# Masked scores written to the ring of probabilities in SBUF, with the exponentials in place there

## The reference, cut to what matters

```
# layer 0: 32 query heads of 16, 8 key/value heads, mask added, bias on every projection
scores = q @ k.T * 16**-0.5 + mask          # 32 x [100, 361]
x = layernorm(softmax(scores) @ v @ Wo + bo + x)
# layer 1: 16 heads of 32 on the normalized context, boolean mask
x = x + tanh(gate) * (softmax(where(mask, q @ k.T * 32**-0.5, -inf)) @ v @ Wo)
```

## Time and profile before

| | us |
|---|---|
| median of 3 executions | 1225.03 |
| the profiled execution, device time | 1223.34 |
| its span in the profile | 1221.5 |
| TensorE matmul busy | 1148.4 (94%) |
| VectorE busy | 806.6 (66%) |
| ScalarE busy | 759.1 (62%) |
| granted TensorE clock, mean | 0.993 |

### The profile page before, as it was taken

The page is one execution under the profiler, slowest core; times in us unless marked ns, Lnnn a source line. Parts: engine busy times, 40 slices in busy tenths (PEclk is TensorE's granted clock), DMA queues, the critical chain, the costliest instruction groups (busy, mean ns, idle before and its releaser), DMA issues.

```text
span 1221.5 us, 32246 instructions
## 1 busy us (share of the span) xinstructions
PE 1148.4 (94%) x10003; PEld 942.6 (77%) x10003; DVE 806.6 (66%) x2370; ACT 759.1 (62%) x2179; POOL 251.6 (21%) x264
## 2 busy tenths in 40 slices
PE   4899999999999999999999999999999999999997
PEld 4678687787878878787887878778787878878786
DVE  4465667667577675757777675767767576675735
ACT  3464756757475675747567474766747476574744
POOL 1042212111121211113121121312122131211210
PEclk9799999999999999999999999999999999999999
DMA  7774627447362744736365482635647273564500
GB/s 237 193 174 99 159 70 173 109 103 190 77 170 69 159 126 101 187 72 163 86 138 147 89 197 64 171 87 127 155 91 189 63 168 91 125 164 94 135 15 8
DMA packets 77965, 153.77 MB, mean 126 GB/s; under 512 B 10528, under 2 KB 47200, under 8 KB 77296
## 3 DMA queue, kind: packets, MB, share of 16 engines
q1 hardware_dynamic: 77936, 153.40, 51.9%
HBM read 113.72 MB, written 39.65 MB: 126 GB/s over the span
## 4 chain that ended last, share of the span: by engine, by line
PE 72%; issue 11%; ACT 7%; DVE 4%; DMA 2%; DVEq 1%; ACTq 1%; SPq 1%; POOL 1%; POOLq 0%
PE PJ L365 16%; PE TP L416 14%; PE SCO L402 6%; PE OA L436 6%; PE SCO L682 5%; PE SCO L460 5%; PE PJ L468 5%; PE PJ L378 4%; ACT PR L1048 3%; PE OA L441 3%; PE SCO L365 2%; ACT PT L1059 2%; DVE SCO L819 2%; PE SCO L406 2%; DVE MN L819 1%
## 5 line engine op out<-in xcount | busy, mean ns | idle before, releaser
L1048 ACT ACTIVATE PR<-SCO,MN 100x361 f32<-100x361 f32 x768 | 426.2, 566 | 147.4 <-DVE MN L819 143.8
L819 DVE CUSTOM_DVE_ANT_0 SCO<-SCO,MK 100x361 f32<-100x361 f32 x768 | 403.0, 550 | 134.8 <-PE SCO L402 102.7
L416 PEld LDWEIGHTS TP<-ident,PR 100*128 100x128 f32 x2304 | 223.1, 141 | 86.8 <-ACT PT L1059 36.9
L416 PE MATMUL TP<-ident,PR 100*128 100x100 f32 x2304 | 270.2, 253 | 10.6 <-ACT PT L1059 4.8
L1059 ACT ACTIVATE PT<-TP 121x600 f32<-121x600 f32 x256 | 171.8, 671 | 49.6 <-PE TP L416 45.7
L402 PE MATMUL SCO<-K0S,Q0S 128*100 128x362 f32 x512 | 161.7, 371 | 32.3 <-ACT PR L1048 26.5
L1048 ACT ACTIVATION_READ_ACCUMULATOR PR<-SCO,MN 100x1 f32 x768 | 158.8, 207 | 0.0
L829 DVE COPY PT<-TP 121x600 f32<-121x600 f32 x128 | 100.1, 782 | 48.8 <-PE TP L416 46.0
L402 PEld LDWEIGHTS SCO<-K0S,Q0S 128*100 128x100 f32 x512 | 74.6, 166 | 56.4 <-ACT PR L1048 47.6
L819 DVE DVE_READ_ACCUMULATOR2_ANT MN<- 100x1 f32 x768 | 109.6, 143 | 0.0
L1217 POOL TENSOR_TENSOR K1F<-K1F,KB 128x364 f32<-128x364 f32 x64 | 50.7, 793 | 279.4 <-DVE K1F L811 278.1
(11 more groups left out here) (140 smaller groups left out, 1813.4 us busy)
## 6 DMA issues: line engine op xcount, KB each, us to landing
K1S<-k_scr SPq DMA_DIRECT2D x128, 364.0 KB, 6.2
k_scr<-K1HL SPq DMA_DIRECT2D x64, 364.0 KB, 2.9
Q0S<-q_scr SPq DMA_DIRECT2D x128, 100.0 KB, 3.9
K0S<-k_scr SPq DMA_DIRECT2D x64, 182.0 KB, 5.0
AT<-ctx_cols SPq DMA_DIRECT2D x16, 722.0 KB, 9.4
V<-ctx_rows SPq DMA_DIRECT2D x16, 484.0 KB
q_scr<-QHL SPq DMA_DIRECT2D x16, 400.0 KB, 2.5
k_scr<-K1HL SPq DMA_DIRECT2D x32, 182.0 KB, 3.0
```

The costliest lines, as they stand in the source:

```text
L416: last = pe.transpose(TP[:, k % 2, c * T:(c + 1) * T], PR[0:T, k % NPR, c * SP:c * SP + P], ident[0:T, 0:T])
L819: dve.tensor_tensor_reduce(out=bank, in0=bank, in1=mask[0:T, :], scale=scale, scalar=3.4e38, op0=ALU.add, op1=ALU.min, accum_out=MN[0:T, k ...
L1048: act.activation(PR[0:T, k % NPR, 0:S], SCO[0:T, k % 3, 0:S], ACT.Exp, bias=MN[0:T, k:k + 1], scale=-1.0, accum_out=SM[0:T, k:k + 1]).then ...
```

## The change

`shift` writes its masked scores into `PR` in SBUF and no longer back into the PSUM bank. It takes over ScalarE's wait for the transposes of pair p - 3. `exps` reads and writes the same buffer of `PR`. TensorE's waits on a bank of `SCO` now ask for the maximum of the tile three before (`shifted`) and not for its exponential (`prob`). VectorE waits once, ahead of its batches, for the zeros that GpSimd puts into `PR`. No line of the diff touches the place of VectorE's copies.

```diff
@@ TensorE, layer 0 (L589)
                         if k >= 3 or not first:
-                            pe.wait_ge(prob, NH * b + k - 2)
+                            pe.wait_ge(shifted, NH * b + k - 2)
                         score(b, k)
@@ TensorE, keys of the next sequence into bank 1 (L646)
-                    pe.wait_ge(prob, NH * b + 32)
+                    pe.wait_ge(shifted, NH * b + 32)
@@ TensorE, layer 1 (L716, L730)
-                        pe.wait_ge(prob, NH * b + 2 * p - 2)
+                        pe.wait_ge(shifted, NH * b + 2 * p - 2)
...
-                        pe.wait_ge(prob, NH * b + 2 * p - 1)
+                        pe.wait_ge(shifted, NH * b + 2 * p - 1)
@@ VectorE, shift (L813)
                 dve.wait_ge(scored, NH * b + k + 1)
+                wait_from(dve, pt_mm, NPAIR * b + k // 2 - 2)
                 dve.sem_inc(met_dve, 1)
-                bank = SCO[0:T, k % 3, 0:S]
                 mask, scale = (MK0, -1.0) if k < 32 else (MK1, -SCALE1)
-                dve.tensor_tensor_reduce(out=bank, in0=bank, in1=mask[0:T, :], scale=scale, scalar=3.4e38,
+                dve.tensor_tensor_reduce(out=PR[0:T, k % NPR, 0:S], in0=SCO[0:T, k % 3, 0:S], in1=mask[0:T, :],
+                                         scale=scale, scalar=3.4e38,
                                          op0=ALU.add, op1=ALU.min, accum_out=MN[0:T, k:k + 1]).then_inc(shifted, 1)
@@ VectorE, ahead of batch 0
+            dve.wait_ge(pool_zero, 3)
@@ ScalarE, exps (L1045)
                 act.wait_ge(shifted, NH * b + k + 1)
-                wait_from(act, pt_mm, NPAIR * b + k // 2 - 2)
-                act.activation(PR[0:T, k % NPR, 0:S], SCO[0:T, k % 3, 0:S], ACT.Exp, bias=MN[0:T, k:k + 1],
+                act.activation(PR[0:T, k % NPR, 0:S], PR[0:T, k % NPR, 0:S], ACT.Exp, bias=MN[0:T, k:k + 1],
                                scale=-1.0, accum_out=SM[0:T, k:k + 1]).then_inc(prob, 1)
```

## The result

The changed kernel takes 1253.8 us (median of 4, 1252.7 to 1254.6) against 1224.9 us for the kernel before on the same chip. The ratio is 1.024, with a 95% interval of 1.022 to 1.025. It is 29 us slower; the forecast was 14 us faster.

The account below looks back on a forecast made before the run. TensorE, with matmuls busy 94% of the span, was taken as the bound. 1.13 - 0.48 + 0.45 - 0.15 = 0.95 us a sequence, times 14, plus 1.0 for batches 0 and 15, is 14.3 us: 1225.0 to 1211, range 1204 to 1218.

Parts of the forecast that it names:

- part (2) of what the change adds: Wait moved from ScalarE to VectorE: never the last met, costs 0 to 0.15 us at idle starts, taken as 0.05.
- Part (3): VectorE's wait for GpSimd's zeros is met long before its first maximum, and the keys' bank wait already was: cost 0.
- The slower rival: Extra wait not hidden on VectorE, 0.12 us on about 20 maxima a sequence: 21 us slower, 1246; chance 0.10.
- The stalls, one by one: Seven score stalls of the loop's sequence, each checked against the next copy wait: 0.40 + 0.46 + 0.40 - 0.13 = 1.13 us kept.
- layer 1: Ring of transposes, VectorE's copy, maximum, exponential and ScalarE's copy, with no score in it: stalls there keep nothing.
- output projection: Behind score 13: starts 0.86 us earlier, when layer 1's outputs are ready; 0.46 us kept in addition to 0.40.
- transposes 7: Behind score 19: of 0.54 us freed, 0.40 is kept, since copy 6 then holds them.
- transposes 9: They hang through ScalarE on maximum 20, which gains only 0.27 us: 0.13 of the 0.40 lost again.
- The waits for ScalarE's copies: Sign of being right: transposes' waits for ScalarE's copies rise from 36.9 us towards 70.
- Exponentials from SBUF: ScalarE's exponentials 30 ns longer each, 16 counting in a sequence: 0.48 us lost, bounds 0.14 and 1.22.
- the nine idle starts of the prediction: Exponentials 0, 4, 8, 16, 20, 24, 35, 40, 44, where idle ScalarE loses its wait: 0.05 us each, 0.45 gained.
- The waits: Per sequence, ScalarE gains 0.45 us at nine idle starts; VectorE loses 0.15 at three (maxima 0, 20 and 26).

Follow-up runs that it names:

- e2: Kernel before, with 20 semaphore increments that nobody waits for on VectorE's queue between batch 0 and its loop: 1267.6 us, ratio 1.035.
- e5: Kernel before, with 17 semaphore increments that nobody waits for ahead of VectorE's loop: 1226.8 us, ratio 1.001.
- e6: Whole changed kernel, with 70 idle increments far ahead in VectorE's queue, where it waits for the first weights: 1206.0 us, ratio 0.985.
- e8: Changed kernel without VectorE's wait for the transposes, and with TensorE's four bank waits set back from `shifted` to `prob`: 1219.0 us, ratio 0.996.
- e1: Changed kernel without VectorE's wait for the transposes, which TensorE's order already implies: 1201.7 us, ratio 0.981.
- e9: Kernel before, without ScalarE's implied wait for the transposes ahead of each exponential: 1219.3 us, ratio 0.996.
- e3: Changed kernel with 60 idle semaphore increments ahead of VectorE's loop: 1211.7 us, ratio 0.989.
- e7: Changed kernel with 40 idle increments far ahead in VectorE's queue, where it waits for the first weights: 1306.2 us, ratio 1.066.
- e4: Kernel before, with 17 idle increments inside VectorE's loop body, in a stretch where VectorE is idle: 1225.1 us, ratio 1.000.

## Why the prediction was wrong

*The failed step* is part (2) of what the change adds: that the moved wait "costs only its place in the queue", at most 0.15 us at a few idle starts. I counted its time and not its instructions, nor where they push the end of VectorE's loop. Part (3) did the same with the wait for GpSimd's zeros: met long before it is needed, it is still one of the two instructions that carry the end from 576 to 578. e2 shows that 20 instructions without any function do the same, e5 that 17 don't, e6 that the changed kernel without the stall takes 1206.0 us. The missing term is +47.8 us. Without slow matmuls the stall costs 73.03 - 70.57 = 2.46 us a pass, of which 2.10 us show as TensorE's wait; the slow matmuls behind eleven of the thirteen returns add 74.37 - 73.03 = 1.34 us each.

*The slower rival* named VectorE's wait and the range up to 1246, but by another mechanism, a price on each of about 20 maxima. It isn't what happened: the wait costs 4.3 us in all, 0.3 us a pass, and the loss sits at one place of a pass.

*The stalls, one by one.* e8 and e1 differ only in the bank waits. Times from the cast of the earlier trace rows on, in e8 and e1:

| point | e8 | e1 | gain | forecast |
|---|---|---|---|---|
| transposes 1 | 22.38 | 22.05 | 0.33 | 0.40 |
| transposes 3 | 26.39 | 26.06 | 0.33 | 0.40 |
| output projection | 28.00 | 27.13 | 0.87 | 0.86 |
| transposes 7 | 36.52 | 35.38 | 1.14 | 1.26 |
| transposes 9 | 40.13 | 39.00 | 1.13 | 1.13 |
| period | 71.39 | 70.24 | 1.15 | 1.13 |

This step was right, layer 1 included: transposes 21 start at 12.94 and 12.97. The waits for ScalarE's copies rose to 64.7 us in e1, where I had said towards 70.

*Exponentials from SBUF.* Drawn, they are 590 - 566 = 24 ns longer each, forecast 30. But two in a row, before and after, start further apart by more than that:

```profile
636.98 0.57 ACT L1048 ACTIVATE PR<-SCO,MN 100x361 f32<-100x361 f32 x1
...
637.52 0.57 ACT L1048 ACTIVATE PR<-SCO,MN 100x361 f32<-100x361 f32 x1
```

```profile
643.03 0.59 ACT L1050 ACTIVATE PR<-PR,MN 100x361 f32<-100x361 f32 x1
...
643.61 0.59 ACT L1050 ACTIVATE PR<-PR,MN 100x361 f32<-100x361 f32 x1
```

That is 0.54 and 0.58 us. Over all exponentials in a row it is 0.535 to 0.553 us before and 0.578 to 0.596 after, 43 ns more, which is the figure that the prediction gives beside its own 30. The cost on the path was mis-sized all the same: I took 0.48 us a pass and set VectorE's side at zero, with bounds of 0.02 us for a maximum, but its accumulator reads end 60 ns earlier. This saving reaches ScalarE: where that had been idle, the exponential starts 0.62 us after the start of its maximum in e9 and 0.57 in e8. At the nine idle starts of the prediction that would be about 0.5 us a pass, an estimate from these two numbers, and so about as much as the 0.48 us that I took for the exponentials. Together, e8 against e9, they gain no more than 0.13 us a pass. No run has one of the two without the other.

*The waits.* ScalarE's loss of its wait: forecast 0.45, measured 71.88 - 71.52 = 0.36. VectorE's wait: forecast 0.15, measured 0.28 (e3) to 0.33 (e6).

Without the stall the sum is 1.15 + 0.36 + 0.13 - 0.33 = 1.31 us a pass, which is 71.88 - 70.57, where I had 0.95; in all the change without the stall (e6) gains 18.9 us, where I had 14.3. The 0.95 was low mainly because the cost of the exponentials was counted and the gain from the accumulator reads wasn't.

## What to carry to other kernels

In a hardware loop, count instructions as well as their time: each wait against a loop's counter may bring an instruction of its own, and a body that comes to touch a third block of 256 instructions costs microseconds at every return, whatever the new instructions do. Instructions ahead of the loop count as well, because they move it. Idle time in the profile that ends with "issue" and occurs once a pass, together with more instruction packets, is the sign; moving the body by idle instructions ahead of it tells place from work. And look for waits that another engine's order already implies: dropping one was worth 5 us in the kernel before, and made the change 23 us faster instead of 29 us slower.

## What the runs showed of the hardware that I had not expected

- A boundary of VectorE's instruction fetch lies ahead of place 321 of its queue (e7) and another ahead of 577 or 578 (e4 and e5 against the changed kernel). A loop body of 316 instructions returns without a stall at 261 to 576, at 323 to 638 and at 333 to 648, and with one at 263 to 578; one of 299 returns with a stall at 281 to 579. Each pass with a stall fetched about (0.63 - 0.11) / 13 = 0.04 MB, and one pass each of the kernel before, e1 and e6 fetched none on q14.
- A TensorE wait of 2.15 us is followed, two microseconds later, by about 3.5 us at the 1.2 GHz level, but one of 2.10 us at another return (1097.94) isn't: the granted clock stays at 1.00. Eleven of the thirteen returns show the lower level. In e7, with two waits close together, the granted clock is 0.50 over the whole of 674 to 683 us.
- Behind a VectorE maximum that writes its tile to SBUF and not to PSUM the accumulator read takes 83 ns and not 143 ns (82 in e8 and 142 in e9, which differ in little but this path).
- Exponentials of 361 columns in a row start 43 ns further apart with their source in SBUF than in PSUM, though each is drawn only 24 ns longer.
